# Turning the gate and up weights on the DMA queue in a one-core convolution and feed-forward kernel

## The reference

```
y    = irfft(rfft(u) * rfft(K))[..., :L] + u * D         # a filter K for each head
y    = y * (arange(L) < length)
q(t) = clip(round(t / s), -128, 127) * s,  s = max(|t|) / 127   # a scale for each row
gate = q(y) @ q(w_gate).T ; up = q(y) @ q(w_up).T        # 2752 x 1024 weights
out  = x + q(silu(gate) * up) @ q(w_down).T              # 1024 x 2752 weights
```

## Time and profile before

| | us |
|---|---|
| median of 3 runs | 1339.59 (1338.51 to 1340.16) |
| profiled execution | 1339.14 |
| its span | 1336.9 |
| PE busy in the span | 1263.6 (95%) |
| DVE / ACT / POOL busy | 918.1 / 409.0 / 345.0 |

### The profile page before, as it was taken

One profiled execution on the slowest core, in us unless ns is written; L12 is line 12 of the kernel. 1 busy time (PEld: TensorE's weight loads), 2 busy tenths in 40 slices (PEclk: granted clock), 3 DMA queues, 4 the chain that ended last, 5 costly groups with the idle time before them and its releaser, 6 DMA issues.

```text
span 1336.9 us, 20250 instructions
## 1 busy us (share of the span) xinstructions
PE 1263.6 (95%) x6837; PEld 686.5 (51%) x6932; DVE 918.1 (69%) x1536; ACT 409.0 (31%) x593; POOL 345.0 (26%) x326
## 2 busy tenths in 40 slices
PE   2499999999996999999999999999999999999997
PEld 0377777776664444444444444444444444444443
DVE  7677877777884865677656777566776567765675
ACT  2244444444451222322222222222222222222322
POOL 3333333324450122221122211222112131122220
PEclk9799999999998999999999999999999999999999
DMA  3279999997974132323323333223332223322323
GB/s 98 75 243 265 273 265 266 271 296 240 264 221 158 32 68 67 71 67 87 74 62 71 71 77 84 61 69 73 78 84 61 69 69 74 86 67 65 71 60 79
DMA packets 137595, 161.52 MB, mean 121 GB/s; under 512 B 101645, under 2 KB 101855, under 8 KB 136287
## 3 DMA queue, kind: packets, MB, share of 16 engines
q1 hardware_dynamic: 137566, 161.16, 44.7%
HBM read 113.28 MB, written 25.49 MB: 104 GB/s over the span
## 4 chain that ended last, share of the span: by engine, by line
PE 67%; issue 0%; DVE 0%; ACT 0%
PE ps_g L1062 23%; PE ps_u L1062 22%; PE ps_o L1088 22%; PE ps_o L1095 1%; PE ps_t L1072 0%; ACT h_t L1197 0%; DVE ps_o L1149 0%; DVE res L1152 0%
## 5 line engine op out<-in xcount | busy, mean ns | idle before, releaser
L1226 POOL TENSOR_TENSOR h_int<-h,rounder 128x512 bf16<-128x512 f32 x186 | 174.4, 952 | 706.2 <-ACT h L1188 703.4
L1062 PE MATMUL ps_g<-wgu,rows 128*128 128x512 bf16 (+1 forms) x1516 | 327.1, 358 | 5.9 <-PEq L413 4.9
L1062 PE MATMUL ps_u<-wgu,rows 128*128 128x512 bf16 (+1 forms) x1493 | 324.4, 356 | 2.3
L1088 PE MATMUL ps_o<-wd,h_t 128*128 128x512 bf16 x1314 | 294.0, 379 | 1.8 <-issue 0.2
L1182 ACT ACTIVATE g_buf<-g_buf 128x512 f32<-128x512 f32 x192 | 112.3, 585 | 583.7 <-DVE g_buf L1120 583.7
L1120 DVE SCALAR_TENSOR_TENSOR g_buf<-ps_g,sx_all,wide 128x512 f32<-128x512 f32 x192 | 132.3, 689 | 229.6 <-PE ps_g L1062 229.6
L853 PE MATMUL ps_y<-u,toep 128*128 128x512 f32 (+7 forms) x1024 | 268.6, 416 | 2.4 <-ACT s_rows L722 1.0
L1062 PEld LDWEIGHTS ps_g<-wgu,rows 128*128 128x128 bf16 x1536 | 145.2, 98 | 163.5 <-issue 13.2
L1062 PEld LDWEIGHTS ps_u<-wgu,rows 128*128 128x128 bf16 x1536 | 147.0, 98 | 151.6 <-issue 1.0
L853 PEld LDWEIGHTS ps_y<-u,toep 128*128 128x128 f32 x1024 | 176.9, 191 | 89.3 <-issue 57.9
L1088 PEld LDWEIGHTS ps_o<-wd,h_t 128*128 128x128 bf16 x1346 | 131.1, 98 | 151.9 <-issue 1.1
(11 more groups left out here) (141 smaller groups left out, 657.6 us busy)
## 6 DMA issues: line engine op xcount, KB each, us to landing
toep<-k_rev SPq DMA_DIRECT2D x64, 512.0 KB, 5.7
res<-in_x SPq DMA_DIRECT2D x64, 256.0 KB, 3.9
out_x<-res SPq DMA_DIRECT2D x64, 256.0 KB, 3.2
wide<-in_L_ffn_w_gate SPq DMA_DIRECT2D x22, 512.0 KB, 6.6
wide<-in_L_ffn_w_up SPq DMA_DIRECT2D x22, 512.0 KB, 8.4
wide<-in_L_ffn_w_down SPq DMA_DIRECT2D x8, 1376.0 KB, 8.5
rows<-in_x SPq DMA_DIRECT2D x32, 256.0 KB, 6.6
x_more<-in_x SPq DMA_DIRECT2D x32, 256.0 KB, 7.0
```

Source lines behind the costliest of these rows:

```text
L1062: last = pe.matmul(bank[:, 0:n], xq[:, par, c, :], wgu[:, NC - 1 - c, first + cols.start:first + cols.stop], start=(c == 0), stop=(c == NC ...
L1088: last = pe.matmul(ps_o[o][:], h_t[0:width, c, :], wd[0:width, c, o * W:(o + 1) * W], start=(c == 0), stop=(c == FC - 1))
L1226: pool.tensor_tensor(h_int[:, piece(j)], h[:, par, piece(j)], rounder[:].to_broadcast([P, n]), ALU.subtract).then_inc(h_int_ready, 1)
```

## The change

Four edits, all in `convolve_and_pack`:

1. **Gate and up weights by the DMA queue.** `turn_w` on PE and `place_w` on ACT are gone for gate tiles. SP issues `dma_start_transpose` of each 128x1024 piece of `w_int` straight into `wgu` (`move_w`), ahead of the gate load and again ahead of the up load. POOL waits for that DMA (`w_moved[k]`) before it writes the piece's place again. Down weights stay on PE and ACT.
2. **Paired input transposes.** `turn_x` turns both heads at once: eight fp32 transposes of 128x128 blocks a tile where there were sixteen of 64x128. `take_u` reorders while it copies, and `u` is double. Both halves are turned right after `convolve(i, 0)`, ahead of `turn_max`.
3. **Order in the down jobs.** PE turns down pieces 0 and 1 before `turn_max(i-1)`, and piece 2 before `spread_inv(i-1)`. ACT does both `take_u`, then place_w 0 and 1, then `round_down`, then place_w 2.
4. **Loops.** The down loop is peeled by one body, and SP's bodies are all written out. SP waits for all gate transposes after tile 22.

```diff
         def move_w(i, k):
+            sp.wait_ge(w_int_ready, pieces(i, k) + 1)
+            first = row_of(i) + k * F
+            sp.dma_start_transpose(wgu[:, :, first:first + P], w_int[:, k * L:(k + 1) * L]).then_inc(w_moved[k], 16)
...
             if gate_stage(i):                       # SP
+                move_w(i, 0)
                 if has(i, GU_ITERS - 2):
-                    sp.wait_ge(w_int_ready, pieces(i, 0) + 1)
                     load_gu(i + 2, par, 0)
...
-            if gate_stage(i) and has(i, GU_ITERS - 2):
-                sp.wait_ge(w_int_ready, pieces(i, 1) + 1)
-                load_gu(i + 2, par, 1)
+            if gate_stage(i):
+                move_w(i, 1)
+                if has(i, GU_ITERS - 2):
+                    load_gu(i + 2, par, 1)
...
+                if gate_stage(i):                   # POOL, unround
+                    if not isinstance(i, int) or i >= 1:
+                        pool.wait_ge(w_moved[k], 16 * i)
...
-            def take_u(i, hh):                      # ACT
-                act.activation(u[:, hh, :], ps_x[hh][:], ACT.Copy).then_inc(u_done, 1)
+            def take_u(i, par, k):
+                act.activation(u[:, par, :, half, :], ps_x[k][:].rearrange("p (c h b) -> p h c b", h=2, b=B),
+                               ACT.Copy).then_inc(u_done, 1)
...
                 if has(i, TILES - 1):
-                    take_u(i + 1, 0)
-                if not gate_stage(i) and has(i, WEIGHT_ITERS - 1):
-                    round_down(i + 1, 1 - par)
+                    take_u(i + 1, 1 - par, 0)
+                    take_u(i + 1, 1 - par, 1)
                 if gate_stage(i):
                     if has(i, GU_ITERS - 1):
                         round_gu(i + 1, 1 - par, 0)
                 elif down_stage(i):
                     place_w(i, par, 0)
                     place_w(i, par, 1)
-                if gate_stage(i):
-                    place_w(i, par, 0)
-                if has(i, TILES - 1):
-                    take_u(i + 1, 1)
+                if not gate_stage(i) and has(i, WEIGHT_ITERS - 1):
+                    round_down(i + 1, 1 - par)
...
-                for c in range(NC):                 # PE, turn_x
-                    last = pe.transpose(ps_x[hh][:, c * B:(c + 1) * B], x_bufs[par][rows, c * P:(c + 1) * P], ident[rows, rows])
+                for c in range(NC // 2):
+                    first = (k * NC // 2 + c) * P
+                    last = pe.transpose(ps_x[k][:, c * P:(c + 1) * P], x_bufs[par][:, first:first + P], ident[:])
...
                     convolve(i, par, hh)            # PE, body
-                    if not last_one:
+                    if not last_one and hh == 0:
                         await_x(i + 1, 1 - par)
+                        for k in range(2):
+                            turn_x(1 - par, k)
+                    if not gate_stage(i) and down_stage(i):
+                        turn_w(i, par, 2 * hh)
+                        if hh == 0:
+                            turn_w(i, par, 1)
...
-                    if not last_one:
-                        turn_x(i + 1, 1 - par, hh)
-                    if gate_stage(i) or down_stage(i):
-                        turn_w(i, par, hh if gate_stage(i) else 2 * hh)
-                        if hh == 0 and not gate_stage(i):
-                            turn_w(i, par, 1)
```

More of the change, by code:

```diff
@@ L461, in convolve_and_pack @@
         w_int_ready = sem("w_int_ready")
+        w_moved = [sem(f"w_moved{k}") for k in range(2)]
         w_turned = sem("w_turned")
@@ L525, in run @@
             stage[0] = "down"
[L526 to L529, removed]
+            body(DOWN_FIRST, DOWN_FIRST % 2)
+            with eng.Fori(DOWN_FIRST + 1, WEIGHT_ITERS - 4, 2) as i:
+                body(i, 1 - DOWN_FIRST % 2)
+                body(i + 1, DOWN_FIRST % 2)
+            for i in range(WEIGHT_ITERS - 3, TILES):
                 body(i, i % 2)
@@ L614, in store_scales @@
                     sp.wait_ge(s_stored, 80)
-            run(sp, body, lambda: store_scales(0))
+            for i in range(DOWN_FIRST):
+                body(i, i % 2)
+            store_scales(0)
+            for k in range(2):
+                sp.wait_ge(w_moved[k], 16 * GU_ITERS)
+            for i in range(DOWN_FIRST, TILES):
+                body(i, i % 2)
             sp.wait_ge(xq_stored, 16 * TILES)
@@ L621, in _, with unround @@
         def _(pool):
-            def unround(i, par, k, turned):
+            def unround(i, par, k):
                 if gate_stage(i):
@@ L638, in unround @@
                                    ALU.subtract).then_inc(w_int_ready, 1)
-            unround(0, 0, 0, None)
+            unround(0, 0, 0)
             def body(i, par):
                 if gate_stage(i):
-                    unround(i, par, 1, pieces(i, 1) - 1 if not isinstance(i, int) or i >= 1 else None)
-                elif down_stage(i):
-                    unround(i, par, 2, pieces(i, 0))
-                if not gate_stage(i) and has(i, WEIGHT_ITERS - 1):
[L648 to L652, removed]
+                    unround(i, par, 1)
+                    if has(i, GU_ITERS - 1):
+                        unround(i + 1, 1 - par, 0)
+                else:
+                    if down_stage(i):
+                        unround(i, par, 2)
+                    if has(i, WEIGHT_ITERS - 1):
+                        unround(i + 1, 1 - par, 0)
+                        unround(i + 1, 1 - par, 1)
             run(pool, body)
@@ L677, in place_w @@
             def place_w(i, par, k):
[L679 to L683 removed]
+                act.wait_ge(w_turned, down_pieces(i, k) + 1)
                 bank = ps_w[(BATCHES * down_slot(par) + k) % 2]
@@ L687, in place_w @@
                 act.activation(wd[:, NC * k:NC * k + whole, cols], bank[:, 0:whole, :], ACT.Copy).then_inc(w_placed, 1)
-            for hh in range(2):
-                take_u(0, hh)
+            for k in range(2):
+                take_u(0, 0, k)
             round_gu(0, 0, 0)
@@ L849, in convolve @@
                 out = ps_y[hh][:].rearrange("p c b -> p (c b)")
+                ahead = u[:, par, hh].rearrange("p c b -> p (c b)")
                 for dist in range(NC):
@@ L852, in convolve @@
                     n = (NC - dist) * B
-                    last = pe.matmul(out[:, dist * B:NC * B], toep[:, slot, block_cols], u[:, hh, 0:n],
+                    last = pe.matmul(out[:, dist * B:NC * B], toep[:, slot, block_cols], ahead[:, 0:n],
                                      start=(dist == 0), stop=(dist == NC - 1), skip_group_check=True)
@@ L887, in _ @@
             await_x(0, 0)
-            for hh in range(2):
-                turn_x(0, 0, hh)
+            for k in range(2):
+                turn_x(0, k)
             def body(i, par):
```

47 lines of the change are left out of this document (20 added, 27 removed).

## The result

The changed kernel took 1317.63 us (median of 4 runs, 1316.20 to 1319.59), beside 1339.73 for the kernel before on the same chip: a ratio of 0.984, 95% interval 0.982 to 0.9855. The profiled execution took 1316.2 us, its span is 1314.2.

The account below looks back on a forecast made before the run. PE was taken to bound gate tiles, DMA close behind, and a loop between maxima the down tiles. From 1339.14 us, +34 for DMA work and -6 for down tiles gave 1367 us; range 1322 to 1393.

Parts of the forecast that it names:

- D: Follow-up account, not in the prediction: in gate tiles the DMA queue is full at 338 GB/s.
- They come back as DMA work: Gate tiles: DMA transposes add 2.60 us to 10.2, making 12.8 us a tile; the stage grows by 34 us.
- Weight transposes leave PE: Gate tiles: PE loses 0.92 us of work in each of 22 tiles, 20.2 us in all.
- Paired input transposes: All tiles: 1.1 us instead of 1.28, near equal; hidden in gate tiles, -0.6 to +0.4 us in the other ten.
- the case that it doesn't pay: Rival: paired transposes take 0.21 us each, 6 us more in ten tiles outside the gate tiles; no separate chance.
- The new order in down tiles: Down tiles: transposes leave the loop between maxima, saving 0.8 us in each of 8 tiles, -6 us, bounds 0 and -9.
- my 11.1: Down tiles: PE's need of about 11.1 us a tile, for convolutions, inputs, weights and small operations.
- the gate-tile step: Gate tiles: DMA engines need 12.8 us, PE would need 9.9, so DMA becomes the bound.
- Rival 1: Gate tiles: DMA engines have room and PE keeps the bound, 1313 us; chance 0.21 with its border.
- rivals 2 and 3: Gate tiles: 2, in-order queue stalls, 1393 us, 0.13 beyond 1385; 3, lowered PE clock, up to 1385, within the 0.56 case.

Follow-up runs that it names:

- one block of eight and the rounding moved: Changed kernel with the xq rounding moved to ScalarE and only one block of eight turned by each gate transpose: 1312.49 us, 0.980.
- the small steps: Changed kernel plus, per gate or up piece, an extra half-piece transpose (1340.31 us) or, separately, an extra plain load of 2 KB rows (1350.00 us).
- the half pieces: Changed kernel with four of each gate and up piece's eight blocks transposed a second time into a spare buffer: 1340.31 us, 1.001.

## Why the prediction was wrong

The reading of what bounds the kernel before was right. The mechanism forecast for after was not: the gate tile is held by VectorE, which the step did not count, and the queue, which was to hold it at 12.8 us, keeps up at 10.0. It may well have no room left there, as D has it, but that is not what sets the time of the changed kernel.

1. **"They come back as DMA work" failed, in both of its figures.** Their sum was to be 12.8 us a tile; the changed kernel moves all of it in 10.02 us or less, and the stage did not grow by 34 us but shrank by 16. The first figure took the busy share for a need: 0.945 x 10.78 = 10.2 us a tile. With one block of eight and the rounding moved, nearly the same bytes fit into tiles of 9.5 us, so the need was at most that; the small steps put it near 8.2, if the queue is full at 10.0. The second figure took a piece at 1.30 us, again by the busy share, on an almost idle queue. At 290 GB/s, which the queue reached with turning packets alone, a piece takes 0.90 us; the half pieces cost 0.93 for one piece's bytes. The share counts those packets for 1.28, so it overstates them even there. The step supported the share with light-load rates of 271 to 315 GB/s of busy time; in the changed kernel whole stretches run at 338 GB/s of real time. The half microsecond at 410 GB/s was the row that told this, and I had used it as a bound only.
The Trainium skill, "DMA: Bandwidth & Descriptors", Latency and other measured facts, has 261 GB/s for a transpose with a non-contiguous middle dimension, by which a piece would take 1.00 us, an estimate. The half microsecond of the changed kernel shows 290 GB/s and the run with half pieces 282, so under load the page of the skill was nearer than my row.

2. **"Weight transposes leave PE", 20.2 us**, was right as PE's own work: an unblocked tile takes 9.15 us, and 10.05 with the transposes back on PE. But it bought nothing beside the other edits, since the tile stopped at 10.0 us, where VectorE holds it.

3. **"Paired input transposes" was mis-sized.** I set about zero and named the case that it doesn't pay as a rival. It saves 0.40 us in the transposes (0.88 us, where I took 1.1), and with the shorter matrix operations around them 0.71 us a tile. The 0.21 us of one transpose alone was a poor bound: eight in a row take 0.11 each.

4. **"The new order in down tiles", 6 us**, came out at 9.3, just over its bound of 9, and partly by another way. The step gave the gain to PE's order, which takes the transposes out of the loop from one maximum to the next. With PE's old order the eight down tiles take 89.96 us, only 2.8 more than in the changed kernel, and PE waits 0.5 us in all for the maximum, where it waited 3.6 before (in five of the eight tiles, not in each as I had read it). The run with ScalarE's old order loses 9.7 us. So it is ScalarE's order that carries the gain, and I hadn't priced it. What the rows show shorter in that loop is the rounding to xq, which no longer lies fully beside POOL's unround (0.73 to 0.83 us in most down tiles instead of up to 2.41). That PE bounds the tile then was right (84.19 of 87.20 us busy); the tiles take 10.90 us on average and 10.39 at the least, below my 11.1 (the terms of which add up to 10.95).

5. **VectorE** was not in the gate-tile step at all, and it is what holds the tile. Its work grew from 8.57 to 9.50 us a tile, 0.91 of it in the rounding to xq, which went from 0.69 to 1.60 us. The rows fit a collision with POOL's unround. Here POOL is at it from 203.61 to 205.50, and the rounding, begun at 204.45, ends 0.55 us after it. In the run with PE's old order the two overlap by 0.45 us (205.15 against a POOL end of 205.60) and it takes 1.00; before, it began at 214.74 and was done as POOL began at 215.42. The end 0.55 us after POOL's is the same in every gate tile of both runs in which the two overlap and POOL ends first. Still, no run took only the overlap away, so this is read, not shown.

6. **Not foreseen: 3.3 us** lost at the start and in tile 22, where x came 1.84 us late and the convolution behind it took 5.80 us instead of 4.11, at a clock of 0.87 over the tile. Rival 1 described the outcome (1313 us) but not its course: PE does not keep the bound in the gate tiles, and that 1317.63 lies so near owes something to luck, the down tiles giving 3 us more than forecast and VectorE taking back about half of what PE had won in the gate tiles (9.15 us of its own work, tiles of 10.02). What rivals 2 and 3 describe, long waits for x and a lowered clock, was seen in the run with the turning twice (clock 0.86), and in small in tile 22 of the changed kernel.

## What to carry to other kernels

A DMA busy share of 0.95 is no evidence that the queue is full: read how many GB/s the densest half microsecond moved, and if the answer decides, add a small transfer and see whether the stage grows. A share is also no price: divide bytes by time in a stretch where only those bytes move. When one bound is taken away, list every engine's need per tile beside it; here PE with all the turning (10.05 us) and VectorE (9.98) stood within 0.1 us of each other, so edits worth 9 and 20 us by themselves were worth 22 together. Before a run is read as relieving an engine, look whether its other operations grew. And work moved to an idle engine is not free if an in-order queue waits for its result.

## What the hardware showed unexpectedly

- The queue's busy share reached 1.08 to 1.09 and stayed there for tiles of 10.0 to 11.4 us; it no longer tells load there.
- 0.26 MB of turning transfers cost 0.93 us a tile under load (282 GB/s; 290 in a half microsecond with nothing else), and 1.30 us by the busy share of smaller ones nearly alone (201 GB/s); plain loads of the same size cost 0.67 us under load.
- Eight fp32 transposes of 128x128 in a row take 0.88 us, 16 of 64x64 took 1.28 us.
- The same rounding on VectorE took from 0.69 to 2.41 us, the longer the more of POOL's unround ran beside it. In gate tiles it ended 0.55 us after the unround, and the 128x128 operation that writes `diag`, 0.29 us alone, ended 0.08 to 0.09 us after it when it was stretched, whether to 0.36 or to 1.97 us.
- After a wait of 1.84 us for x in tile 22 of the changed kernel, the next convolution took 5.80 us at a lowered clock. In the run with the turning twice, from 105 to 246 us, waits of 1.83 and 2.28 us left it at 4.11 us and waits of 2.6 us and more did not.
